# A two-layer transformer on one core: a third bank pair for the gate layer, openings that use idle PSUM banks, and selection's first loads issued inside the stage before it

## The chip, the cores and the metric

One core of one Trainium2 chip runs the whole program. The metric is the device time of one execution in microseconds (us), lower is better. A measurement of this kernel can tell some 0.2% (4 us) from no change.

## What is computed

A tensor x of 8 batches x 512 rows x 256 channels, float32, passes through two layers.

```
xn = layernorm(x)
x  = x + attention0(xn) + ffn0(xn)       # causal, 16 heads of 16, keys and values from a latent of 64
xn = layernorm(x)                        # ffn0: silu(w1 x) * (w2 x) -> gelu(h1 .) -> gelu(h2 .) -> w3, 1024 hidden
x  = x + attention1(xn) + ffn1(xn)       # attention1: no mask, a position bias per head from a table
# ffn1, per group of 16 rows: for each of 64 experts pick the row with the largest logit (controller),
#   inner = relu(f1[expert] row + bias), inter = f2[expert] inner, and add inter back to the picked row
```

Products are made of float32 values split in a rounded high part and a low part (the rest), each a float32r operand.

## The kernel before, in words

The program is a row of five stages, each one block in which every engine has its own instruction stream: attention of layer 0 (`latent_attention`), its feed-forward (`layers`), attention of layer 1 (`biased_attention`), selection (`choose`) and the experts with the final sum (`apply`). A stage begins on all engines once the one before has ended on all of them. The tiles of a stage lie in SBUF over those of earlier stages.

**Attention stages.** Both run a list written out by hand, `STEADY`: 32 steps with events placed in them (`placed`), offset so that a turn holds parts of three batches. Each engine walks the list in the same order and emits its own part of each event. Per batch: the normalized rows are turned by TensorE (`x_turn`), split in high and low (`xh`, `xl`), stored for later stages by SP, multiplied with the weights (`latent` and `qk` in layer 0, four `qk` products in layer 1), and the queries and keys split again into `parts`. SP copies these with six DMAs per group of four heads (`stack`) into `stacks`, from which the score products read. A score is made twice: once for its maximum (`score`, read by VectorE), once for the exponential (`prob`). TensorE's outputs rotate over three slots of two PSUM banks.

- Layer 0, start of a batch (lines 364 to 376, 449 to 466, 319 to 326): ScalarE copies the slot to `x_full` (L368), VectorE rounds it into `xh` (L452), GpSimd subtracts to get `xl` (L321). The queries and keys go the same way through `qk_full`: L375, L463, L324. The third engine of each chain releases the next product or SP's `stack` DMAs (L286).
- Layer 1, start of a batch: the two `x_turn` (L1066) and the four `qk` (L1058) all go through one bank, `single`, since the three slots are in use by the batch before. ScalarE rounds out of it (L941, L947), VectorE subtracts (L1003, L1006), and only then may TensorE write the next one. In the opening batch no earlier batch uses the three slots.

After the `stack` DMAs of two groups SP issues the load of the next batch's rows, `x_load` (L272, L875).

**Feed-forward.** `pe_batch` issues for each of eight blocks of 128 hidden units a gate product and an up product of 8 matmuls in all (L1290), into one of two bank pairs, `gates[o % 2]`, `ups[o % 2]`. Before block o it waits for `gate_done` of block o - 2. ScalarE takes the tanh (L1240), VectorE forms `gated` (L1261) and `full` (L1266, `gate_done`), ScalarE rounds it (L1244, L1247), GpSimd makes the low part (L1232). Two hidden layers of 8 x 16 matmuls (L1320) and the output product (L1366) follow. Banks 0, 1 hold gates, 2, 3 ups, 4 to 7 are free in the gate layer, 4, 5, 2, 3 serve the hidden layers, 6, 7 the output. In batch 0 ScalarE also rounds the weights as they arrive (L1448). In the last batch TensorE computes layer 1's bias table beside the gate layer; its first product waits for the load of `c_fir` (L1183).

**Selection.** Loads of the controller and four constants are issued by ScalarE, those of `xh`, `xl`, `xn` of a batch by SP, at the start of the stage. For each batch: logits (six matmuls, L1989), tie added, maximum and `perm` on VectorE (L1953, L1956, L1960), turned by TensorE (L1996), masked blocks (L1970), and the selecting products (L2009, L2010) from `th` and `tl`, the high and low part of `xn` (ScalarE L1931, GpSimd L1908). The stage of attention 1 ends with ScalarE waiting until its last store of the attention output has landed.

Of the kernel before, what the change touches and what calls it, by code (L numbers as in the profile page):

```python
# [96 lines left out]
def latent_attention(nc, x_d, out_d, xh_d, xl_d, w, c, sems, front):  # L97
# [4 lines left out]
    with ExitStack() as ctx:  # L102
# [163 lines left out]
        with nc.Block() as block:  # L266
# [47 lines left out]
            def _(pool):  # L314
                def emit(kind, b, n, i):
                    if kind == "ln_rstd":
                        wait(pool, eps_done, 1, b)
                        nc.gpsimd.tensor_tensor(rstd[:], var_eps[:], power[:], ALU.pow).then_inc(rstd_ready.sem, 1)
                    if kind == "x_low":
                        wait(pool, xh_ready, 1, b)  # L320
                        pool.tensor_tensor(xl[:], x_full[:], xh[:].bitcast(F32), ALU.subtract).then_inc(xl_ready.sem, 1)  # L321
# [20 lines left out]
            def _(act):  # L342
# [21 lines left out]
                def emit(kind, b, n, i):  # L364
                    if kind == "x_copy":
# [6 lines left out]
                    if kind == "qk_copy":  # L372
                        wait(act, qk_ps, n + 1, b)
                        wait(act, low_ready, n, b)
                        act.copy(qk_full[:], slot("qk", n)[:]).then_inc(qk_copied.sem, 1)  # L375
                        if n == 1 and opening(b):
                            more_high_weights()
# [35 lines left out]
            def _(dve):  # L413
# [18 lines left out]
                def emit(kind, b, n, i):  # L432
# [16 lines left out]
                    if kind == "x_high":  # L449
# [9 lines left out]
                    if kind == "qk_high":  # L459
# [4 lines left out]
                        if n == 1 and opening(b):  # L464
                            more_low_weights()
# [169 lines left out]
def biased_attention(nc, x_d, out_d, xh_d, xl_d, xn_d, w, c, sems, used, x_stored):  # L635
# [4 lines left out]
    with ExitStack() as ctx:  # L640
# [5 lines left out]
        def sem(name, per=0, grant=0, unit=1):  # L646
# [34 lines left out]
        consts_in, w_in = sem("consts_in", unit=16), {n: sem(f"w_in_{n}", unit=16) for n in names + ("o",)}  # L681
        bias_in = [sem(f"bias_in{g}", unit=16) for g in range(QUADS)]
        blank, keyed, ones_ready, w_high, w_ready = \
            sem("blank"), sem("keyed", unit=16), sem("ones_ready"), sem("w_high"), sem("w_ready")
        x_loaded, x_saved = sem("x_loaded", 1, unit=16), sem("x_saved", 2, unit=16)
        xn_saved = sem("xn_saved", 1, unit=16)
        stats_done, moments_done, xn_ready = sem("stats_done", TT), sem("moments_done", TT), sem("xn_ready", TT)
        shift_ready = sem("shift_ready", 1)
        eps_done, rstd_ready = sem("eps_done", 1), sem("rstd_ready", 1)
        xt_ps, xh_ready, xl_ready = sem("xt_ps", KD), sem("xh_ready", KD), sem("xl_ready", KD)  # L690
        v_ps, v_ready = sem("v_ps", 1), sem("v_ready", 1)
        qk_ps, high_ready, low_ready = sem("qk_ps", 4), sem("high_ready", 4), sem("low_ready", 4)
        stack_in = [sem(f"stack_in{g}", 6, unit=16) for g in range(QUADS)]
        tops_in = [sem(f"tops_in{g}", 2, unit=16) for g in range(QUADS)]
        a_ps, a_max = sem("a_ps", STEPS), sem("a_max", STEPS)
        m_ps, tops_ready = sem("m_ps", QUADS), sem("tops_ready", QUADS)
        b_ps, p_exp = sem("b_ps", STEPS), sem("p_exp", STEPS)
        p_copied, p_pooled, p_added = sem("p_copied", STEPS * 3 // 4), sem("p_pooled", STEPS * 3 // 4), sem("p_added", STEPS // 4)
        value_ps, o_copied, ot_ps = sem("value_ps", QUADS * TT), sem("o_copied", QUADS), sem("ot_ps", QUADS)
        inv_ready, mix_ready = sem("inv_ready", QUADS), sem("mix_ready", QUADS)  # L700
        mt_ps, mh_ready, ml_ready = sem("mt_ps", KD), sem("mh_ready", KD), sem("ml_ready", KD)
        out_ps, out_ready = sem("out_ps", 1), sem("out_ready", 1)
        out_saved = sem("out_saved", 1, grant=1, unit=16)
        held_sp, held_dve = sem("held_sp"), sem("held_dve")


        STEADY = []
        def later(s):
# [1656 lines left out]
```

## Time and profile before

| | us |
|---|---|
| three runs | 2061.07, 2060.01, 2056.81; median 2060.01 |
| profiled execution, its own time | 2058.57 |
| span of its profile | 2056.8 |
| TensorE busy, VectorE, ScalarE, GpSimd | 1773.8 (86%), 1148.1, 1063.8, 983.4 |
| attention 0 | 0 to 496 |
| feed-forward | 496 to 1187, a batch of the middle six in 83 |
| attention 1 | 1192 to 1857, a batch in some 78 |
| selection | 1857 to 1920 |
| experts and sum | 1921 to 2057 |

The stages are the stretches between the last instruction of one block and the first of the next in the timeline. Busy times are of the span; TensorE's clock is given in each window as the share that was granted (1.00 is 2.4 GHz, 0.50 is 1.2 GHz). A row of the timeline gives start, duration, engine, line, operation, output and inputs, how many were merged, and in brackets the idle time of the engine before it with what ended that.

### The profile page before, as it was taken

What the parts mean: (1) busy time and instruction counts of PE and PEld (TensorE: products, weight loads), DVE (VectorE), ACT (ScalarE), POOL (GpSimd) and SP (SyncE); (2) the same over time, 40 slices, a digit from 0 to 9 for tenths busy, and PEclk for the clock granted to TensorE, in tenths of its full rate; (3) what the DMA queues carried; (4) which work ended last, traced back from release to release, by engine and by line L of the source; (5) the groups of instructions that cost most, each with busy time, mean ns of one, the idle gap of its engine ahead of it and who ended that gap; (6) DMA issues with size and microseconds to landing.
All of it is one profiled execution on the core that took longest, in us unless ns stands there. A gap on an engine that the chain in (4) does not pass through costs nothing. (4 is left out here: it accounts for less than half of the span.)

```text
span 2056.8 us, 34075 instructions
## 1 busy us (share of the span) xinstructions
PE 1773.8 (86%) x11015; PEld 1141.0 (55%) x11015; DVE 1148.1 (56%) x2519; ACT 1063.8 (52%) x1455; POOL 983.4 (48%) x739
## 2 busy tenths in 40 slices
PE   4888888887999999999997958878878878866999
PEld 2455555544878788787885833334334334325566
DVE  5666666662253353443533358877877877935335
ACT  1555555555432232222322218877877877964542
POOL 3444444432343434434342427776766876954202
PEclk7999999998999999999998959989989989977999
DMA  3333332325420111110201362132132222107346
GB/s 111 94 104 96 94 102 84 96 58 165 150 72 24 56 54 48 56 47 33 79 23 45 115 193 85 57 80 83 60 80 84 62 72 82 32 11 277 122 152 212
DMA packets 119236, 182.53 MB, mean 89 GB/s; under 512 B 14197, under 2 KB 73077, under 8 KB 119162
## 3 DMA queue, kind: packets, MB, share of 16 engines
q1 hardware_dynamic: 109228, 170.45, 27.2%
q10 hardware_dynamic: 9296, 9.05, 1.3%
q0 software_dynamic: 640, 2.10, 0.3%
q8 instruction: 42, 0.69, 0.1%
q14 instruction: 30, 0.25, 0.0%
HBM read 90.72 MB, written 39.91 MB: 64 GB/s over the span
## 5 line engine op out<-in xcount | busy, mean ns | idle before, releaser
L808 POOL TENSOR_TENSOR l_prob<-l_prob,l_bias 128x1024 f32<-128x1024 f32 x192 | 452.2, 2375 | 147.5 <-ACT l_prob L960 146.6
L1232 POOL TENSOR_TENSOR f_hl<-f_full,f_hh 128x512 fp32r<-128x512 f32 x192 | 247.9, 1291 | 426.2 <-DVE f_hh L1270 271.2
L1019 DVE CUSTOM_DVE_ANT_0 l_slot<-l_slot,l_bias 128x512 f32<-128x512 f32 x512 | 340.8, 716 | 52.0 <-PE l_slot L1093 50.0
L963 ACT ACTIVATE l_prob<-l_prob 128x1024 f32<-128x1024 f32 x256 | 271.1, 1071 | 0.0
L472 DVE TENSOR_REDUCE l_peak<-l_slot 128x2 f32<-128x256 f32 (+3 forms) x256 | 206.3, 821 | 107.3 <-PE l_slot L564 105.0
L1320 PE MATMUL f_ps<-f_hh,f_hi_h 128*128 128x512 f32 x1024 | 259.9, 390 | 1.5 <-ACT f_hh L1244 1.1
L1320 PE MATMUL f_ps<-f_hl,f_hi_h 128*128 128x512 f32 x1024 | 258.3, 389 | 0.0
L388 ACT ACTIVATE l_prob<-l_slot 128x1024 f32<-128x1024 f32 (+3 forms) x256 | 174.7, 705 | 97.9 <-PE l_slot L583 95.2
L1320 PEld LDWEIGHTS f_ps<-f_hh,f_hi_h 128*128 128x128 f32 x1024 | 192.1, 188 | 44.1 <-ACT f_hh L1244 2.1
L1320 PEld LDWEIGHTS f_ps<-f_hl,f_hi_h 128*128 128x128 f32 x1024 | 192.2, 188 | 39.9
L960 ACT COPY l_prob<-l_slot 128x1024 f32<-128x1024 f32 x192 | 194.7, 1014 | 35.7 <-PE l_slot L1109 34.9
L1252 ACT ACTIVATE f_full<-f_ps,f_h_s 128x512 f32<-128x512 f32 x128 | 86.8, 684 | 235.2 <-PE f_ps L1320 216.2
L334 POOL TENSOR_SCALAR_AFFINE_SELECT l_prob<-l_prob 128x256 f32<-128x256 f32 x256 | 105.2, 418 | 210.2 <-ACT l_prob L388 207.4
L1270 DVE CAST f_hh<-f_full 128x512 fp32r<-128x512 f32 x128 | 62.1, 485 | 256.3 <-ACT f_full L1252 255.2
L1093 PE MATMUL l_slot<-l_stacks 63*128 63x512 f32 x512 | 120.7, 471 | 47.8 <-DVE l_prob L808 23.5
L1123 PE MATMUL l_o_bank<-l_prob,l_vals 128*32 128x512 f32 x1024 | 157.1, 690 | 4.5 <-ACT l_prob L963 4.5
L1109 PE MATMUL l_slot<-l_stacks 64*128 64x512 f32 x512 | 135.4, 527 | 22.3 <-DVE l_peak L1019 16.2
L1109 PEld LDWEIGHTS l_slot<-l_stacks 64*128 64x128 f32 x512 | 51.7, 200 | 140.5 <-DVE l_peak L1019 98.3
L559 PE MATMUL l_slot<-l_stacks 63*128 63x256 f32 (+2 forms) x512 | 98.6, 382 | 32.7 <-ACT l_prob L388 17.6
L583 PE MATMUL l_slot<-l_stacks 64*128 64x256 f32 (+2 forms) x512 | 109.8, 428 | 11.0 <-DVE l_peak L472 4.0
L1240 ACT ACTIVATE f_tanh<-f_ps,f_gate_s 128x512 f32<-128x512 f32 x64 | 43.9, 687 | 138.3 <-PE f_ps L1290 138.3
L597 PE MATMUL l_o_bank<-l_prob,l_vals 128*32 128x512 f32 (+3 forms) x1024 | 97.9, 454 | 11.1 <-POOL l_prob L334 9.7
(210 smaller groups left out, 2827.0 us busy)
## 6 DMA issues: line engine op xcount, KB each, us to landing
l_stacks<-l_parts SPq DMA_DIRECT2D x384, 128.0 KB, 2.6
attn<-l_out_sb ACTq DMA_DIRECT2D x16, 512.0 KB, 2.9
f_raw<-in_L_ffn_h_w SPq DMA_DIRECT2D x16, 512.0 KB, 4.1
f_raw<-in_L_ffn_h_w SPq DMA_DIRECT2D x32, 256.0 KB, 2.6
e_w<-in_L_ffn_f SPq DMA_DIRECT2D x32, 256.0 KB, 2.9
l_bias<-ext SPq DMA_DIRECT2D x16, 448.0 KB, 8.1
l_x_in<-in_L_attn_x SPq DMA_DIRECT2D x8, 512.0 KB, 3.8
xh<-l_xh SPq DMA_DIRECT2D x8, 512.0 KB, 2.6
```

Of the source, the lines that this page charges most:

```text
L388: act.activation(prob[:, n // 2 % RING, 2 * pr:2 * pr + 2, j * P:T], slot(kind, n)[:, :, j * P - q0:wide], ACT.Exp).then_inc(p_exp.sem, 1)
L472: dve.tensor_reduce(peak[:, g, :, pr, t], slot(kind, n)[:, :, 0:(t + 1) * P], AX_X, ALU.max)\
L583: ins = pe.matmul(out[:, a, 0:wide], stacks[r, 1, 2 * g + pr, j * P:(j + 1) * P], stacks[r, 0, 2 * g + pr, q0:T], start=True, stop=True)
L808: return eng.tensor_tensor(probs(n), src, bias[:, h:h + 2, j * P:j * P + T], ALU.add)
L960: act.copy(probs(n), slot(kind, n)[:]).then_inc(p_copied.sem, 1)
L963: act.activation(probs(n), probs(n), ACT.Exp).then_inc(p_exp.sem, 1)
L1019: ins = dve.tensor_tensor_reduce(src, src, bias[:, 4 * g + 2 * pr + a, t * P:t * P + T], 1.0, 3 * NEG, ALU.add, ALU.max, peak[:, g, a, pr, ...
L1093: ins = pe.matmul(out[:, a], stacks[r, 0, 2 * g + pr, t * P:(t + 1) * P], stacks[r, 1, 2 * g + pr, ::-1], start=True, stop=True)
L1109: ins = pe.matmul(out[:, a], stacks[r, 1, 2 * g + pr, j * P:(j + 1) * P], stacks[r, 0, 2 * g + pr, ::-1], start=True, stop=True)
L1123: ins = pe.matmul(o_bank[32 * a:32 * a + 32, :], vals_sb[:, v0:v0 + 32], prob[:, n % RING, a], start=(j == 0), stop=(j == TT - 1), skip_gr ...
L1232: pool.tensor_tensor(t.hl[layer % 2][:, o], t.full[:, n % 2], t.hh[layer % 2][:, o].bitcast(F32), ALU.subtract).then_inc(self.h_lo.sem, 1)
L1320: ins = pe.matmul(t.hidden[n % 4][:], t.hi[m][:, k, cut], src[layer % 2][:, k], start=first and k == 0, stop=last and k == KH - 1, skip_gr ...
```

## The change

1. Gate layer: three pairs of banks (the third is banks 4, 5); the wait is for block o - 3; the hidden layer's first product waits for block 5 of the gate layer; the bias table's products move from banks 4, 5 to 6, 7.
2. Attention 1, opening batch only: the two `x_turn` write into the two banks of slot 2, the four `qk` into the four banks of slots 0 and 1, without waiting for one another. The first score waits until all four `qk` have been split.
3. Attention 0, opening batch only: ScalarE rounds straight out of PSUM into `xh` and `parts`, VectorE subtracts straight out of PSUM. GpSimd's `x_low` and `qk_low` and the copies to `x_full` and `qk_full` are left out there.
4. Selection: SP issues the controller, the first batch's `xh`, `xl`, `xn` and the constants at the end of its stream of attention 1, after the last `v` copy and the last `stack` DMAs; VectorE splits the controller there too. The wait for the last store moves from the end of attention 1 to the start of selection's ScalarE and the end of its SP. Tiles `xh`, `xl`, `xn` of selection become one per slot and lie in another order.

```diff
 # latent_attention
-                    if kind == "x_copy":
+                    if kind == "x_copy" and opening(b):
+                        wait(act, xt_ps, 1, b)
+                        act.copy(xh[:], slot("x_turn", 0)[:]).then_inc(xh_ready.sem, 1)
+                    elif kind == "x_copy":
...
+                    if kind == "x_high" and opening(b):
+                        wait(dve, xh_ready, 1, b)
+                        dve.tensor_tensor(xl[:], slot("x_turn", 0)[:], xh[:].bitcast(F32), ALU.subtract)\
+                           .then_inc(xl_ready.sem, 1)
+                        wait(dve, xl_ready, 1, b)
+                        dve.sem_inc(xt_full.sem, 1)
...
+                    if kind == "qk_high" and opening(b):
+                        wait(dve, high_ready, n + 1, b)
+                        dve.tensor_tensor(parts[:, n, 0:4:3], slot("qk", n)[:], parts[:, n, 1:3].bitcast(F32),
+                                          ALU.subtract).then_inc(low_ready.sem, 1)
 # biased_attention
+    def bank(kind, n, b):
+        if not opening(b):
+            return single[:]
+        return slots[2][:, n] if kind == "x_turn" else slots[n // 2][:, n % 2]
...
                     if kind == "x_turn":
-                        claim(SINGLE, 1, kind, n, i)
+                    if not opening(b):
+                        claim(SINGLE, 1, kind, n, i)
...
+                    if n == 0 and opening(b):
+                        wait(pe, low_ready, 4, b)
...
             clears(sp, used)
+            sp.wait_ge(v_ready.sem, v_ready.at(1, B - 1))
+            for g in range(QUADS):
+                sp.wait_ge(stack_in[g].sem, stack_in[g].at(6, B - 1))
+            next_opening.sp(sp)
...
-                act.wait_ge(out_saved.sem, out_saved.at(1, B - 1))
...
+            next_opening.dve(dve)
 # Layers
-            if o >= 2:
-                pe.wait_ge(self.gate_done.sem, self.gate_done.at(o - 1, i))
-            two = [t.gates[o % 2][:], t.ups[o % 2][:]]
+            if o >= 3:
+                pe.wait_ge(self.gate_done.sem, self.gate_done.at(o - 2, i))
+            two = [t.gates[o % 3][:], t.ups[o % 3][:]]
...
+                if n == 0:
+                    pe.wait_ge(self.gate_done.sem, self.gate_done.at(KH - 2, i))
...
-        t.gates, t.ups, t.hidden, t.outs = psum[0:2], psum[2:4], psum[4:6] + psum[2:4], psum[6:8]
+        t.gates, t.ups, t.hidden, t.outs = psum[0:2] + psum[4:5], psum[2:4] + psum[5:6], psum[4:6] + psum[2:4], psum[6:8]
...
-        table = BiasTable(nc, sb, f.sem, *bias, c, [psum[4], psum[4], psum[5]],
+        table = BiasTable(nc, sb, f.sem, *bias, c, [psum[6], psum[6], psum[7]],
 # choose
+        def open_sp(sp):
+            sp.dma_start(w_raw[:], controller.rearrange("(k p) n -> p k n", p=P)).then_inc(w_in.sem, 16)
+            load_rows(sp, 0, 0)
+            sp.dma_start(xn[0][:], xn_d[0]).then_inc(xn_in[0].sem, 16)
+            for dst, src in ((tie, "c_tie"), (group, "c_group"), (ident, "c_ident"), (parity, "c_parity")):
+                sp.dma_start(dst[:], c[src]).then_inc(consts_in.sem, 16)
...
             @block.scalar
             def _(act):
-                act.dma_start(w_raw[:], controller.rearrange("(k p) n -> p k n", p=P)).then_inc(w_in.sem, 16)
-                for dst, src in ((tie, "c_tie"), (group, "c_group"), (ident, "c_ident"), (parity, "c_parity")):
-                    act.dma_start(dst[:], c[src]).then_inc(consts_in.sem, 16)
+                act.wait_ge(opening_of.last_saved.sem, opening_of.last_saved.at(1, B - 1))
```

## Rows read from the trace of the kernel before

**Rows 1.** Windows, one feed-forward batch: us, busy by engine, granted clock, DMA share, GB/s

```profile
670.00:753.00 83.00, 81.41 (x386) 67.30 (x385) 33.59 (x65) 23.90 (x39) 33.29 (x25) 1.00 0.16 49
```

**Rows 2.** Timeline of TensorE in the gate layer of batch 1

```profile
586.85 1.09 PE L1290 MATMUL f_ps<-f_xl,f_hi_w 128*128 128x512 f32 x4
...
591.14 1.20 PE L1290 MATMUL f_ps<-f_xl,f_hi_w 128*128 128x512 f32 x4 [0.47 <-DVE f_full L1266]
...
603.92 1.96 PE L1320 MATMUL f_ps<-f_hh,f_hi_h 128*128 128x512 f32 x7
```

**Rows 3.** Line 1290, batches 1 to 6, idle of matmul and weight load: us, times

```profile
  DVE f_full L1266: 26.5, 36
```

**Rows 4.** Timeline of ScalarE and VectorE, block 0 of that gate layer

```profile
588.89 0.69 ACT L1240 ACTIVATE f_tanh<-f_ps,f_gate_s 128x512 f32<-128x512 f32 x1 [11.77 <-PE f_ps L1290]
...
590.33 0.75 DVE L1266 SCALAR_TENSOR_TENSOR f_full<-f_ps,f_both_s,f_gated 128x512 f32<-128x512 f32 x1
```

**Rows 5.** Timeline of TensorE, end of batch 0's gate layer

```profile
518.37 0.47 PE L1320 MATMUL f_ps<-f_hh,f_hi_h 128*128 128x512 f32 x1 [1.06 <-ACT f_hh L1244]
```

**Rows 6.** Timeline of TensorE, the last batch's gate layer

```profile
1107.61 0.51 PE L1183 MATMUL f_ps<-f_wpos,f_coeffs 4*101 4x16 f32 x2 [14.51 <-DMA f_out_sb<-c_fir]
```

**Rows 7.** Timeline of VectorE, GpSimd and TensorE in attention 0's opening, the x split

```profile
14.23 0.69 DVE L452 CAST l_xh<-l_x_full 128x1024 fp32r<-128x1024 f32 x1 [1.83 <-ACT l_x_full L368]
...
15.01 2.34 POOL L321 TENSOR_TENSOR l_xl<-l_x_full,l_xh 128x1024 fp32r<-128x1024 f32 x1 [5.36 <-DVE l_xh L452]
...
17.49 0.76 PE L513 MATMUL l_m_bank<-l_xl,l_wc 128*128 128x512 f32 x1 [4.34 <-POOL l_xl L321]
```

**Rows 8.** Timeline there: first stack DMAs, first score, next x; a VectorE sum from PSUM

```profile
27.24 7.91 SPq L286 DMA_DIRECT2D l_stacks<-l_parts  x12
...
33.48 0.58 PE L559 MATMUL l_slot<-l_stacks 63*128 63x256 f32 x2 [8.59 <-issue]
...
39.43 0.43 DVE L436 BATCH_NORM_STATS2 l_stats<-l_x_in 128x6 f32<-128x256 f32 x1 [2.54 <-DMA l_x_in<-in_L_attn_x]
...
1821.58 1.23 DVE L808 TENSOR_TENSOR l_prob<-l_slot,l_bias 128x1024 f32<-128x1024 f32 x1 [5.28 <-PE l_slot L1109]
```

**Rows 9.** Timeline of attention 1's opening batch, and one window (columns as Rows 1)

```profile
1194.67 1.11 PE L1066 MATMUL l_single<-l_ident,l_xn 128*128 128x128 f32 x4 [1.40 <-DVE l_xl L1003]
1197.28 0.77 PE L1058 MATMUL l_single<-l_xl,l_wq 128*128 128x512 f32 x1 [1.49 <-DVE l_xl L1003]
...
1201.62 0.77 PE L1058 MATMUL l_single<-l_xl,l_wk 128*128 128x512 f32 x1 [1.45 <-issue]
...
1205.90 7.89 SPq L891 DMA_DIRECT2D l_stacks<-l_parts  x12
...
1214.48 0.69 DVE L1019 CUSTOM_DVE_ANT_0 l_slot<-l_slot,l_bias 128x512 f32<-128x512 f32 x1
...
1218.33 0.43 DVE L990 BATCH_NORM_STATS2 l_stats<-l_x_in 128x6 f32<-128x256 f32 x1
...
1209.00:1213.00 4.00, 2.68 (x6) 1.82 (x6) 0.69 (x1) 0.49 (x1) 0.00 (x0) 0.50 0.75 201
```

**Rows 10.** Timeline across the end of attention 1 and the start of selection

```profile
1853.87 0.39 ACTq L978 DMA_DIRECT2D attn<-l_out_sb  x1
1857.24 0.47 ACTq L1924 DMA_DIRECT2D s_w_raw<-in_L_ffn_controller  x1
...
1863.23 0.77 PE L1989 MATMUL s_ps<-s_xl,s_w_high 128*128 128x512 f32 x1 [10.49 <-DMA s_xl<-yl]
...
1868.53 0.69 DVE L1953 TENSOR_TENSOR s_logits<-s_ps,s_tie 128x512 f32<-128x512 f32 x1 [5.99 <-DMA s_parity<-c_parity]
...
1868.58 2.34 POOL L1908 TENSOR_TENSOR s_tl<-s_xn,s_th 128x1024 fp32r<-128x1024 f32 x1 [31.65 <-DMA s_parity<-c_parity]
...
1869.98 1.49 DVE L1960 TENSOR_TENSOR s_perm<-s_logits,s_best 128x512 f32<-128x512 f32 x1
...
1871.52 1.12 PE L1996 MATMUL s_ps<-s_ident,s_perm 128*128 128x128 f32 x4 [5.39 <-DVE s_perm L1960]
```

More of the change, by code:

```diff
@@ L371, in emit @@
                         act.copy(top[:], m_bank[:]).then_inc(c_top.sem, 1)
-                    if kind == "qk_copy":
+                    if kind == "qk_copy" and opening(b):
+                        wait(act, qk_ps, n + 1, b)
+                        act.copy(parts[:, n, 1:3], slot("qk", n)[:]).then_inc(high_ready.sem, 1)
+                    elif kind == "qk_copy":
                         wait(act, qk_ps, n + 1, b)
@@ L758, in slot @@
-        def slot(kind, n):
-            return slots[[(u[0], u[2]) for u in PAIRED].index((kind, n)) % 3]
-        def there(b):
-            return not isinstance(b, int) or 0 <= b < B
-        def turns(eng, emit):
-            def turn(i):
-                for kind, off, n in STEADY:
-                    if there(i + off):
-                        emit(kind, i + off, n, i)
-            turn(-1)
-            turn(0)
-            with eng.Fori(1, B - 1) as i:
-                turn(i)
-            turn(B - 1)
-            turn(B)
@@ new lines, in biased_attention @@
+    for s in range(STEPS):
+        STEADY += placed[s]
+        STEADY.append(("prob", 0 if s >= LAG else -1, (s - LAG) % STEPS))
+        at = s - LAG - TAKEN
+        STEADY.append(("prob_exp", 0 if at >= 0 else -1, at % STEPS))
+        STEADY.append(("score", 0, s))
+    LAST_READ = {"score": a_max, "prob": None, "v": v_ready, "out": out_ready,
+                 "maxima": tops_ready, "x_turn": xl_ready, "qk": low_ready, "heads_turn": mix_ready, "mix_turn": ml_ready}
+    PAIRED = [e for e in STEADY if e[0] in ("score", "prob", "v", "out")]
@@ new lines, in bank, with there, turns, turn @@
+    def bank(kind, n, b):
+        if not opening(b):
+            return single[:]
+        return slots[2][:, n] if kind == "x_turn" else slots[n // 2][:, n % 2]
+    def there(b):
+        return not isinstance(b, int) or 0 <= b < B
+    def turns(eng, emit):
+        def turn(i):
+            for kind, off, n in STEADY:
+                if there(i + off):
+                    emit(kind, i + off, n, i)
+        turn(-1)
+        turn(0)
+        with eng.Fori(1, B - 1) as i:
+            turn(i)
+        turn(B - 1)
+        turn(B)
```

912 lines of the change are left out of this document (465 added, 447 removed).

## The prediction

> **What bounds the kernel now.** I read the busy shares first, then the granted clock by slices, then the timeline of each place that the diff touches, and for the gate layer the idle time of its line. The five stages run one after the other, so every microsecond saved on the path inside one comes off the whole. In the feed-forward TensorE is the bound: busy 81.41 of 83 us of a batch at a granted clock of 1.00 [rows 1]. What it loses there it loses in the gate layer, waiting for VectorE [rows 2, 3]. The three other edits lie where one batch alone is under way, and nothing else covers a wait: a chain over three engines at the opening of attention 0 [rows 7], one PSUM bank passed from hand to hand at the opening of attention 1 [rows 9], and loads that are issued only once the stage before has ended [rows 10].
>
> **Part 1, the gate layer.** Eight blocks of 8 matmuls take from 586.85 to 603.92, 17.07 us [rows 2]. Blocks 0 and 1 run without a wait. Their 16 matmuls end 0.47 before 591.14, after 3.82 us, and the first four of them take 1.09 [rows 2]; so twelve more cost 2.73, 0.228 each, a block of eight is 1.83 and eight blocks are 14.6. The stage thus loses 2.4 us, in three waits (36 entries for matmul and weight load together are 18 waits in six batches [rows 3]). A wait is the chain of block o: tanh 0.69 from 588.89, `gated`, `full` up to 591.08, and TensorE starts at 591.14 [rows 2, 4]. From the end of a block's products to `gate_done` that is 2.3 us. With two pairs it must fit in one block, 1.83; with three it has two blocks, 3.66, and 1.3 us to spare. Do the other engines keep up with a block every 1.83? ScalarE has the tanh (0.69) and a rounding of the same size, VectorE 0.69 and 0.75, each under 1.5, so the wait goes and none takes its place. The new wait ahead of the hidden layer asks for block 5, which was done over a microsecond before TensorE comes to it: nothing. The start of the hidden layer waits for the rounding of block 6 and does so at the same distance from the end of the gate layer. Batches 1 to 6: 6 x 2.4 = 14.6 us.
> Batch 0 gives nothing. ScalarE rounds weights between the tanhs there, and TensorE stands 1.06 us waiting for its rounding at the end of the gate layer [rows 5]; reaching that wait earlier makes it longer. The last batch gives nothing either: TensorE waits 14.51 us for the table of `c_fir` [rows 6], a load issued behind the store of batch 6, and the waits saved ahead of it are taken back by it. The table's move to banks 6 and 7 costs nothing: their reader, the output of batch 6, is done before block 3. Bounds: 13.0 (a tenth lost in new small waits) and 14.8.
>
> **Part 2, attention 0's opening.** Now a copy on ScalarE ends where VectorE starts at 14.23; then 0.69 for the cast, 2.34 on GpSimd, and TensorE starts at 17.49 [rows 7]. After, ScalarE's copy is the rounding, of the same size, and VectorE subtracts from PSUM: 1.23 for 1024 elements, one operand from PSUM [rows 8]. It ends at 15.46, TensorE starts at 15.6: 1.9 us less. The same exchange for the queries and keys takes 1.9 more off the moment at which SP issues its stack DMAs, 27.24 now [rows 8]. Scores need the first six of these (33.48, 6.24 after the first issue), and the load of the next rows is issued behind all twelve and is waited for at 39.43 [rows 8]. Both hang on SP's start, so the whole stage moves by up to 3.8. GpSimd was idle else, and what is left out there covers nothing. Bounds 3.2 (the products between lie at 1.2 GHz, and the clock may rise no earlier than it did) and 3.9. I take 3.7.
>
> **Part 3, attention 1's opening.** The second `x_turn` waits 1.40 for the bank and follows at once after [rows 9]. The first `qk` then starts 1.4 earlier, at 1195.9; its own wait of 1.49 for the second split stays. From one `qk` to the next is 4.34, of which 1.45 idle [rows 9]. SP's first stack DMAs need `qk` 0 and 1: 1.4 + 1.45 and some 0.3 because the second is no longer behind a drained pipeline, 3.2 us: 1202.7 instead of 1205.90. From there it is as in attention 0: scores 6.24 later at 1208.9, VectorE's first maximum at about 1209.8 instead of 1214.48, 4.7 earlier. But the next rows are issued behind twelve DMAs of 7.89 in all and land 4.3 after that (39.43 against 27.24 + 7.91 [rows 8]), at 1214.9, and VectorE wants them after three scores. So VectorE, ahead of plan, waits for them, and the stage moves by what separates 1214.9 from 1218.33 [rows 9], 3.4. The new wait of the first score for all four splits costs nothing: these are done by 1208.5, the stack DMAs land later. Behind it in TensorE's queue stands nothing else of that batch. I take 3.5; bounds 3.0 and 4.7.
> The granted clock is 0.50 in this stretch and TensorE was busy 2.68 of 4 us [rows 9]. With the four products in one run it may rise within them, which takes up to 1 us more off. The Trainium skill, in "TensorE: Matmul & The Clock Gate", section "Why this matters for your kernels", says that idle gaps between bursts of matmuls send the array back to the low clock; by that rule the run without gaps would be shortened and part 3 would be 4.3 in place of 3.5.
>
> **Part 4, selection's loads.** Now: last store issued at 1853.87, next stage's first issue at 1857.24, logits at 1863.23 (waiting for `xl`), VectorE at 1868.53 (waiting for the last constant, `parity`), turn of `perm` at 1871.52 [rows 10]. After, batch 0's data and the constants are in SBUF long before, as SP is free once the last stacks are made, and the stage turns over when ScalarE has issued the store: 1853.87 + 0.39 and some 0.4, 1854.7. Six logit products at 1.2 GHz are 2.9 (4.34 - 1.45 [rows 9]): 1857.6. VectorE then needs 1.45 up to `perm` (1868.53 to 1869.98 [rows 10]): 1859.0.
> Here a new order counts. ScalarE's `th` waits for the last store, which lands at about 1857, so GpSimd's `tl` runs from some 1858.1 to 1860.5 (2.34 [rows 10]). In the trace `perm` beside it took 1.49 and ended at 1871.47, 0.55 after GpSimd's 1870.92. I let it end 0.55 after GpSimd again, 1861.0, and the turn starts at 1861.1: 10.4 us earlier. The Trainium skill, "SBUF — State Buffer", section "SBUF: two separate sides", says that a VectorE instruction with two SBUF inputs and a GpSimd one exclude each other by a lock on a shared port pair; this trace agrees with its 1.49 for `perm`, and without such a lock this part would be 11.2.
> What is late next: batch 1's `xh`, `xl` and `xn`, issued by SP from 1854.7 on, behind one another and with the first expert weights. They have 6.4 us to the turn at 1861.1; today the first two loads of the stage, with the constants beside them, take from 1857.24 to 1863.23 [rows 10], 6.0. So they are just in time, and `xn` is wanted last. SP's seven new issues (about 0.4 us each [rows 10]) lie in its idle time; VectorE's split of the controller stands behind its last instruction while TensorE and ScalarE still work. Both cost nothing; were that cover gone, 3 and 0.8 us. Bounds: 8.5 (batch 1 late by 2) and 13 (logits still at the high clock, `perm` ahead of GpSimd). I take 10.4.
>
> **Sum.** 14.6 + 3.7 + 3.5 + 10.4 = 32.2 us. The profiled execution took 2058.57, so 2026.4 of its kind; it lies 1.4 under the median of the runs, 2060.01, so 2027.8 for a median.
>
> **Rivals.**
> A. *The gate's waits move* instead of going: ScalarE or GpSimd falls behind, TensorE waits at the third pair or at the hidden layer. For it: three engines follow one another. Against: each has under 1.5 of work in 1.83 [rows 4]. Half of the gain would be left: 2035.
> B. *Selection is bound by batch 1's loads.* Traffic then sets the pace at its start, and part 4 gives 5 rather than 10: 2033. For it: `xl` and `parity` are waited for today [rows 10]. Against: 1.5 MB fewer are in the queue.
> C. *Slower.* Attention 1 falls into another rhythm, since its opening hands VectorE work 3 to 5 us earlier than the loads for the next batch, with TensorE at 0.50 of its clock [rows 9] for longer in each of the seven batches that follow. It decides from 4.6 us per batch on (32.2 / 7); at 6 the time is 2070. Nothing in the profile shows a batch that depends on how the first began.
> Within the forecast, with a chance of 0.3: the clock rises inside the four `qk` products, which is worth up to 1 us, 2027 instead of 2027.8.
> D. *The openings' edits do not act* (another wait ends at the same time, such as weights or the bias load): parts 2 and 3 give nothing, 2035.
>
> **How the numbers follow.** Forecast 0.76, A 0.07, B 0.09, C 0.02, D 0.06. The range takes in the bounds, 8.5 + 13.0 + 3.0 + 3.2 = 27.7 to 13 + 14.8 + 4.7 + 3.9 = 36.4, that is 2032.3 to 2023.6, widened by the runs' own spread of 2 to each side (2056.81 to 2061.07), and on the slow side up to A, B and D: 2021 to 2035. Faster by over 0.2% (4 us; what a measurement of this kernel can tell from no change): all but C, 0.97. Within 0.2%: 0.01. Slower: 0.02.
>
> **What would show it.** Line 1290 without waits for `full` in batches 1 to 6 and a batch in 80.6 instead of 83; TensorE's first latent product at 15.6 and SP's stacks at 23.4; four `qk` products in one run, stacks 3 to 4 us sooner after the start of attention 1; no wait for a constant in selection, and 7 us from the last store's issue to the turn of `perm` instead of 17.6. It would be wrong if L1290 waits for anything in those batches, if attention 1's batches are longer than today, or if selection's second batch waits for its `xh` or `xn`.

## The result, and the profile after

Six runs of the changed kernel took 2048.42, 2039.23, 2040.68, 2049.53, 2040.46 and 2039.73 us, median 2040.57; six of the kernel before beside them had a median of 2059.43. The ratio is 0.9916 (95% interval 0.9900 to 0.9932): faster by 0.84%. Between the medians it is 18.9 us; the ratios here and below differ a little from those of the medians. Forecast were 32.2 us and 2027.8, with a range of 2021 to 2035. So 13 us are missing, and the median lies 5.6 us outside the range. The profiled execution is the one of 2048.42, span 2046.7. Five of the executions behind the tables below were in a slower state of the chip, 5 to 54% longer, and all medians leave them out.

The four places that the diff touches do what it says. First windows of both kernels: a feed-forward batch of the changed one, then all of attention 1 in the kernel before (us, busy by engine, granted clock, DMA share, GB/s).

```profile
670.00:750.48 80.48, 80.48 (x386) 67.67 (x385) 33.62 (x66) 23.97 (x39) 33.35 (x25) 1.00 0.16 50
```

```profile
1190.00:1860.00 670.00, 526.00 (x2912) 235.76 (x2912) 495.21 (x1320) 508.06 (x589) 462.58 (x203) 0.88 0.25 73
```

TensorE is busy for the whole batch, where it was for 81.41 of 83 [rows 1]. The timeline of TensorE in the gate layer of batch 1 answers to [rows 2]:

```profile
588.45 1.09 PE L1326 MATMUL f_ps<-f_xl,f_hi_w 128*128 128x512 f32 x4
...
602.08 1.08 PE L1326 MATMUL f_ps<-f_xh,f_hi_w 128*128 128x512 f32 x4
602.99 1.96 PE L1356 MATMUL f_ps<-f_hh,f_hi_h 128*128 128x512 f32 x7
```

Eight blocks now take 14.54 us (588.45 to 602.99), forecast 14.6, and no row between bears a wait. Next come the openings: attention 0's subtraction, first stacks and first score, as in [rows 7, 8], then attention 1's, as in [rows 9].

```profile
14.23 1.22 DVE L460 TENSOR_TENSOR l_xl<-l_slot,l_xh 128x1024 fp32r<-128x1024 f32 x1 [1.83 <-ACT l_xh L369]
...
15.61 0.77 PE L534 MATMUL l_m_bank<-l_xl,l_wc 128*128 128x512 f32 x1 [2.45 <-DVE l_xl L460]
...
23.61 6.61 SPq L286 DMA_DIRECT2D l_stacks<-l_parts  x10
...
29.78 0.58 PE L580 MATMUL l_slot<-l_stacks 63*128 63x256 f32 x2 [6.65 <-issue]
...
1177.99 1.94 PE L1098 MATMUL l_slot<-l_ident,l_xn 128*128 128x128 f32 x8 [5.12 <-PEq L1643]
1181.42 0.77 PE L1089 MATMUL l_slot<-l_xl,l_wq 128*128 128x512 f32 x1 [1.49 <-DVE l_xl L1033]
1181.99 1.05 PE L1089 MATMUL l_slot<-l_xh,l_wq 128*128 128x512 f32 x2
...
1187.94 0.62 PE L1089 MATMUL l_slot<-l_xh,l_wk 128*128 128x512 f32 x2
1194.43 1.65 PE L1128 MATMUL l_slot<-l_stacks 63*128 63x512 f32 x6 [5.87 <-DMA l_stacks<-l_parts]
...
1200.42 0.43 DVE L1020 BATCH_NORM_STATS2 l_stats<-l_x_in 128x6 f32<-128x256 f32 x1 [1.06 <-DMA l_x_in<-x]
```

TensorE's first latent product is at 15.61 instead of 17.49, the first stack DMA at 23.61 instead of 27.24, the first score at 29.78 instead of 33.48: 3.7 us. In attention 1 the four `qk` follow one another without a wait, and VectorE waits 1.06 us for the next rows, as forecast. And the turn into selection, as in [rows 10]:

```profile
1855.78 0.39 ACTq L1009 DMA_DIRECT2D attn<-l_out_sb  x1
...
1856.80 0.77 PE L2052 MATMUL s_ps<-s_xl,s_w_high 128*128 128x512 f32 x1 [2.15 <-PEq L894]
...
1860.31 2.34 POOL L1979 TENSOR_TENSOR s_tl<-s_xn,s_th 128x1024 fp32r<-128x1024 f32 x1 [20.48 <-ACT s_th L2000]
...
1861.25 1.95 DVE L2023 TENSOR_TENSOR s_perm<-s_logits,s_best 128x512 f32<-128x512 f32 x1
...
1863.26 0.85 PE L2059 MATMUL s_ps<-s_ident,s_perm 128*128 128x128 f32 x4 [3.56 <-DVE s_perm L2023]
```

From the last store's issue to the turn of `perm` it takes 7.48 us, where it took 17.65 (1853.87 to 1871.52).

Yet look at the last store itself: 1855.78, later than the 1853.87 of [rows 10], though attention 1 began 14 us earlier. So the loss lies inside attention 1. ScalarE's copies of a batch's output (line 974 before, 1005 after) are good marks. Before, the first is at 1351.8 and the eighth at 1852.8, 501.0 us apart; after, 1335.6 and 1854.7, 519.1 apart. The first six follow one another every 78.5 us before and every 82.2 after (82.16 is (1746.4 - 1335.6) / 5). No line of that loop's steady batches was changed. The granted clock of all of attention 1 does not give the cause away: here is the same window after, with the same 0.88 (the columns are those of the second window above). Over the five steady batches alone, from the first output copy to the sixth, it is 0.91 before and 0.89 after, a difference to which the experiments come back.

```profile
1190.00:1860.00 670.00, 523.15 (x2886) 235.85 (x2886) 491.74 (x1315) 506.50 (x584) 459.80 (x199) 0.88 0.24 71
```

### The profile page after: what moved, and what is told of

Its sections match the earlier page's. It is cut to its first block and busy times, and to the rows that moved or that the text cites. A ratio compares the mean times of both kernels' runs of the same rounds, so it can differ in the third digit from the quotient of the medians.

```text
span 2046.7 us, 34076 instructions
## 1 busy us (share of the span) xinstructions
PE 1773.9 (87%) x11015; PEld 1149.2 (56%) x11015; DVE 1150.4 (56%) x2519; ACT 1066.1 (52%) x1455; POOL 978.8 (48%) x736
## 5 line engine op out<-in xcount | busy, mean ns | idle before, releaser
L1128 PE MATMUL l_slot<-l_stacks 63*128 63x512 f32 x512 | 125.0, 488 | 61.5 <-DVE l_prob L835 27.4
L1144 PEld LDWEIGHTS l_slot<-l_stacks 64*128 64x128 f32 x512 | 52.8, 204 | 138.7 <-DVE l_peak L1049 85.1
L1128 PEld LDWEIGHTS l_slot<-l_stacks 63*128 63x128 f32 x512 | 54.4, 209 | 101.1 <-DVE l_prob L835 41.7
```

Of the source, the lines that this page charges most:

```text
L1128: ins = pe.matmul(out[:, a], stacks[r, 0, 2 * g + pr, t * P:(t + 1) * P], stacks[r, 1, 2 * g + pr, ::-1], start=True, stop=True)
L1144: ins = pe.matmul(out[:, a], stacks[r, 1, 2 * g + pr, j * P:(j + 1) * P], stacks[r, 0, 2 * g + pr, ::-1], start=True, stop=True)
```

## Experiments

My first theory, T1, came from the low stretches of the granted clock, which in the changed kernel fall on other products of a batch: the loop keeps a rhythm with the clock, and whatever shifts its start throws it into another one. T2: the new opening of attention 1 itself makes the batches longer. T3: changed addresses or the early loads do. The mean batch in the tables is a fifth of the time from the first to the sixth output copy, in the run's profile. A median of the kernel before taken beside each group stands with it. "First to last" is the distance of those eight output copies in the run's profile.

**One part at a time** (before: 2059.19). Each run has the lines of one part of the diff, and the lines before for the rest.

> Only part 1 of the change (the gate layer on three pairs of banks); openings and selection as before. All theories: the gate stage is shorter by 6 x 2.5 = 15 us. Theory T1 (the attention loops keep a rhythm with the ups and downs of the granted clock, and what is shifted ahead of them can throw them into another one): attention 1, whose own code is that of before, starts 15 us earlier and may now take 80 to 82 us a batch where it took 78.2 (up to 18 us lost of the 15 won; 2042 to 2062), with a clock dip more per batch; if it keeps 78.2, 2045. Rival T2 (the new opening of attention 1 by itself puts the loop into the worse rhythm): 2044 to 2046, batches of 78.2 us. Rival T3 (selection's early loads or the changed addresses slow attention 1): the same 2044 to 2046.

> Only part 2 (attention 0's opening split from PSUM). All theories: first score product and first layer-norm wait 3.6 us earlier. T1: the batches' spacing in attention 0 changes by a us or two each, so that 0 to 3.6 us of it is left at that stage's end, and attention 1 may fall into either of its spacings (78.2 or 81.9 us): anything from -4 to +18 us against before, and runs of two kinds. T2 and T3: the 3.6 us stay, 2056, with attention 1 at 78.2 us a batch.

> Only part 3 (attention 1's opening batch round six score banks). T2: the batches of attention 1 take 81.9 us as in the changed kernel, and the whole is slower than before by some 14 us (2073). T1: the spacing may be either; first store 3 to 4.7 us earlier. T3: batches of 78.2 us, 2056.

> Only part 4 (selection's constants loaded in the drain of attention 1). T1: nothing ahead of selection's own loads is moved, so attention 1 keeps its 78.2 us a batch; the stretch from the last out copy of attention 1 to the end of the span is shorter by 10 to 12 us, 2048 to 2050. T2: the same. T3: the changed addresses alone give attention 1 batches of about 82 us, so that the whole is no faster than before (2055 to 2065).

| run | median us | ratio (95%) | mean batch of attention 1 | first to last |
|---|---|---|---|---|
| gate_only | 2047.42 | 0.9944 (0.9931 to 0.9957) | 78.7 | 500.7 |
| open0_only | 2072.59 | 1.0056 (1.0037 to 1.0074) | 81.4 | 516.5 |
| open1_only | 2057.46 | 0.9986 (0.9976 to 0.9996) | 79.0 | 503.2 |
| select_only | 2050.64 | 0.9955 (0.9942 to 0.9968) | 78.6 | 501.1 |

The second part, the opening of attention 0, makes the kernel 13 us slower by itself, and does so in attention 1, 1.2 ms after its own instructions. That rules out T2 and T3: part 4 leaves the batches alone, and part 3 makes them 0.5 longer, not 3.7. It left T1 standing, for the wrong reason.

**Without the second part, and with a filled or delayed attention 1** (before: 2059.30). `three_parts` has `OPEN0` off. The other two edits are these; `warm` issues two products at each of the first places and four at each of the other two. Those that write to `single` also wait until that bank's last reader is done, which the lines shown leave out.

```diff
 # warm: after each of the first eight scores, ahead of each wait for tops_in, ahead of ml_ready
+pe.matmul(out, wq[:, 0, 0, 0:P], wv[:, 0, 0], start=True, stop=True)
 # delay: ScalarE, opening batch of attention 1, before the first copy of x_turn; three times
+act.copy(o_sb[:, 0], wq[:, 0].bitcast(F32).rearrange("p k d -> p (k d)")).then_inc(lagged.sem, 1)
+act.wait_ge(lagged.sem, m + 1)
```

> The change without its second part (attention 0's opening as before). The three parts alone gave -11.8, -1.7 and -8.6 us, in sum -22.1. Additive parts: 2037, 3.5 us under the changed kernel although one improvement is taken out of it. T1 (rhythm of attention 1 with the granted clock): the batches of attention 1 may take 78 to 79 us (then 2033 to 2038) or 81 to 82 (then 2048); with the second part's own 3.6 us at the start missing, any time under the changed kernel's 2040.6 speaks for T1 against T2, since the opening of attention 1 is still the new one.

> The kernel before, with products whose result nobody reads put into TensorE's idle time in attention 1 from its second batch on: two of 256 columns behind each score product of the first eight steps of a batch, four ahead of the wait for each quad's maxima, four ahead of the output product. They cost 48 x 0.11 = about 5 us of TensorE's time a batch where they don't fit into waits. T1: what makes a batch 78 to 82 us is the stretches at the low clock, so with these filled the granted clock of attention 1 rises from 0.88 to 0.95 or more and the batches fall to 74 to 77 us: 10 to 25 us less, 2035 to 2050. If the low clock is only a by-product and VectorE and ScalarE set the batch, the clock rises and the time stays or grows: 2059 to 2080.

> The changed kernel with the same filling products. T1: its 81.9 us a batch and those of the kernel before fall to the same 74 to 77 us, so that the four parts show nearly their whole sum: 2005 to 2030, 28 to 32 us under the filled kernel before. T2 (the new opening makes the batches longer by itself): still 3 to 4 us a batch slower than the filled kernel before.

> The changed kernel with ScalarE held up by three copies (about 2 us) between attention 1's first turn product and the copy of it, nothing else. Without a rhythm: 2 us slower, 2042.5. T1: the loop meets the clock's fall at another place, and the time moves by something else than 2 us: from 10 us faster to 10 us slower, with another spacing of the batches than 81.9 us, or with runs spread wider than the changed kernel's.

| run | median us | ratio (95%) | mean batch | first to last |
|---|---|---|---|---|
| three_parts | 2032.33 | 0.9880 (0.9857 to 0.9902) | 78.5 | 500.1 |
| warm_before | 2083.83 | 1.0110 (1.0086 to 1.0133) | 81.7 | 519.6 |
| warm_after | 2065.85 | 1.0034 (1.0016 to 1.0052) | 85.1 | 536.2 |
| delay3_after | 2042.54 | 0.9922 (0.9900 to 0.9944) | 80.8 | 513.3 |

Three parts are 8 us faster than all four. The filling is a miss for T1: in the kernel before the clock of the steady batches (1430 to 1745) rose from 0.91 to 0.93, and the batches grew by 3 us. The 260 filling products in the trace kept TensorE busy for 58.3 us, 0.22 each where I had set 0.11, and it stood idle ahead of some of them (8.2 us in all, nearly all of it until VectorE had written `l_mix`); which of the two made the batches longer was not taken apart. Filled before and filled after still lie 3.4 us a batch apart; but their clocks in that window, 0.93 and 0.90, differ as well, so this pair alone doesn't decide. And the delay of 1.92 us made the whole 2.0 us longer.

**Delays with and without the second part** (before: 2063.44). `all_wait0` puts six such copies ahead of attention 0's first rounding; the others put two, five and six into attention 1. T4 is new: it is the second part's code, and not when it runs. (T5, tried against it further down: it is something else that the second part leaves behind.)

> The changed kernel, all four parts, with ScalarE held up by six copies (6 x 0.64 = 3.8 us by the copies of the last delayed run) between attention 0's first turn product and its first rounding, so that its first score product stands where it stood before the second part (33.5 us) while the second part's code stays. T1 (what counts is where the loops meet the clock's falls, hence when they start): the batches of attention 1 go back to 76.6 to 80.3 us and the whole to that of the three parts, 2030 to 2038, that is 3 to 10 us faster for 3.8 us of added waiting. Rival T4 (the second part's code, its addresses or its order slows something later by itself, whenever it runs): 2044, batches of 80.5 to 82 us.

> The three parts (without attention 0's new opening) with ScalarE held up by two copies (1.3 us) at the start of attention 1. T4: 1.3 us slower than the three parts, 2033.6, same batches of 76.6 to 80.3 us. T1: another meeting with the clock; batches of 80 to 82 us are possible though the second part is absent, 2030 to 2050.

> The same with five copies (3.2 us). T4: 2035.5, same batches of 76.6 to 80.3 us. T1: 2030 to 2050, and the three times at 0, 1.3 and 3.2 us of delay don't lie on the line of slope 1.

> The changed kernel, all four parts, with six copies (3.8 us) at the start of attention 1; three copies gave 2042.5 with batches of 80.5 to 81.1 us. T4: 2044.4, batches of 80.5 to 82 us. T1: the phase may be that of the fast rhythm: 2033 to 2050, batches of 76.6 to 80.3 us possible though the second part is in.

| run | median us | ratio (95%) | mean batch | first to last |
|---|---|---|---|---|
| all_wait0 | 2047.02 | 0.9922 (0.9907 to 0.9937) | 81.2 | 513.5 |
| three_wait2 | 2033.46 | 0.9858 (0.9839 to 0.9877) | 78.3 | 501.8 |
| three_wait5 | 2035.11 | 0.9860 (0.9841 to 0.9879) | 79.0 | 503.2 |
| all_wait6 | 2048.26 | 0.9917 (0.9896 to 0.9938) | 81.9 | 518.6 |

T1 has fallen. Without the second part, delays of 0, 1.3 and 3.2 us give 2032.3, 2033.5 and 2035.1 and batches of 78.3 to 79.0. (That the three times lie on a line of slope 1 shows little: the kernel before took 4 us more beside the last two than beside the first.) With it, no delay brings a batch below 80.8. Attention 0's first score back near its old place (33.07) didn't help.

With that I read what the idle time of VectorE in attention 1 is put down to, kernel by kernel. Waits of VectorE from 1190 to 1860, total us, times, longest; first `three_parts`, then the changed kernel:

```profile
DVE l_slot L1056 <- PE l_slot L1136: 55.2, 33, 5.1
...
DVE l_slot L1056 <- issue: 0.7, 3, 0.4
```

```profile
DVE l_slot L1049 <- PE l_slot L1128: 62.9, 35, 5.5
...
DVE l_slot L1049 <- issue: 9.4, 3, 3.4
...
DVE l_prob L835 <- issue: 3.9, 5, 0.9
```

"Issue" is time in which the engine waited for nothing that the profile shows. Every kernel with the second part up to here has five such gaps in line 835 (3.2 to 3.9 us in all) and most have some of 3 us before line 1049; none without it has more than 0.7 us in all. In VectorE's timeline the gaps of 3 us stand at one place, where a turn of its loop ends and the next one begins. The loop has six turns, so it jumps back five times. The changed kernel:

```profile
1418.90 0.73 DVE L1049 CUSTOM_DVE_ANT_0 l_slot<-l_slot,l_bias 128x512 f32<-128x512 f32 x1
...
1422.63 0.70 DVE L1049 CUSTOM_DVE_ANT_0 l_slot<-l_slot,l_bias 128x512 f32<-128x512 f32 x1 [2.94 <-issue]
...
1425.05 1.23 DVE L835 TENSOR_TENSOR l_prob<-l_slot,l_bias 128x1024 f32<-128x1024 f32 x1 [0.88 <-issue]
```

TensorE's score for the row at 1422.63 had begun at 1420.33. In `three_parts` the first of the same two rows of VectorE starts 0.69 us after its score, and the second right behind the copy of the maxima:

```profile
1573.57 0.50 PE L1136 MATMUL l_slot<-l_stacks 63*128 63x512 f32 x2 [1.23 <-ACT l_prob L996]
```

```profile
1574.26 0.70 DVE L1056 CUSTOM_DVE_ANT_0 l_slot<-l_slot,l_bias 128x512 f32<-128x512 f32 x1 [1.31 <-PE l_slot L1136]
...
1575.52 0.27 DVE L1065 CAST l_tops<-l_single 16x128 fp32r<-16x128 f32 x1
1575.75 1.22 DVE L839 TENSOR_TENSOR l_prob<-l_slot,l_bias 128x1024 f32<-128x1024 f32 x1
```

The totals put down to "issue" are too small, for the profile names TensorE for some of these gaps. Read at the row itself, whatever is named, a long gap is there at all five jumps of every kernel with the second part. These are the ranges over all twenty profiles, the later ones included; the loop's place is explained below, and so is why the kernels fall into four groups by it.

| loop begins at | profiles | gap at the jump, us | second gap, before the addition (line 835) |
|---|---|---|---|
| 829, 845, 848 | 11 | 1.31 to 1.37 | none put down to "issue" |
| 832 | 7 | 2.94 to 3.78 | 0.60 to 0.93 |
| 833 | 1 | 2.87 to 2.95 | 0.70 to 0.72 |
| 840 | 1 | 4.20 to 4.45 | none |

Behind the sixth turn, where nothing jumps back, it is 1.09 in all twenty. In the changed kernel the gaps sum to 19.7 us and in the kernel before to 7.1. So 12.6 of the 18.1 us by which attention 1 is longer stand in these rows. The rest goes with the clock. From the first to the sixth output copy the granted clock is 0.91 or 0.92 in all ten kernels of the first group that have no filling products. It is 0.91 in `delay3_after`, whose attention 1 is the least lengthened of the others, 0.87 to 0.89 in the other seven, and lowest in `all_pad8`, the longest. That the gaps bring the clock down, and that the lower clock costs the rest, fits these numbers but was not tried by itself.

One more row of the page differs: the packets of the second instruction queue. It is the page's section on DMA queues (packets, MB, share), kernel before first, changed kernel second.

```profile
q8 instruction: 42, 0.69, 0.1%
q14 instruction: 30, 0.25, 0.0%
```

```profile
q14 instruction: 55, 0.45, 0.1%
```

So the changed kernel fetches 0.20 MB more of instructions, 25 packets for five jumps back. In the built program VectorE's loop of attention 1 is 268 instructions long. It begins at number 829 of VectorE's queue in the kernel before, and at 832 in the changed one, because the second part puts three bare `sem_inc` on that queue. ScalarE's loop is 172 long and lies one place earlier, GpSimd's is 52 long and lies three places earlier, and TensorE's, 412 long, did not move.

**Moving the loop's code** (before: 2058.86; for `all_pad8` and `all_pad16` 2059.59). The fillers cost nothing, VectorE idles there.

```diff
 # VectorE, attention 1, ahead of turns(dve, emit); 3, 1, 13, 8 or 16 times
+dve.sem_inc(lagged.sem, 1)
 # all_moved: the three increments of the second part go from VectorE to GpSimd, for x:
-wait(dve, xl_ready, 1, b)
-dve.sem_inc(xt_full.sem, 1)
+wait(pool, xl_ready, 1, b)
+pool.sem_inc(xt_full.sem, 1)
 # and the two of qk_copied behind low_ready in the same way
```

> The three parts (no new opening in attention 0) with three increments of a semaphore that nobody waits for, put on VectorE's queue right ahead of its turns in attention 1. VectorE idles there, so they cost nothing themselves; with them its loop of attention 1 (268 instructions) begins at instruction 832 of its queue, where it begins with the second part, and not at 829. T4 as it now reads (VectorE stands still for 3 us with nothing that it waits for, where its loop of attention 1 turns back, in every kernel with the second part and in none without, because of where the loop's code lies): the idle time put down to issue comes up here too, batches of 80.5 to 82 us, 2040 to 2048. T5 (it is something else that the second part leaves behind, on ScalarE, GpSimd or in the data): no change, 2032, batches of 76.6 to 80.3 us.

> All four parts with one such increment: the loop begins at 833. T4, if only certain places are bad (832 is the first multiple of 4, of 16 and of 64; 829 leaves 1, 13 and 61): the gap of 3 us goes if a multiple of 4 or more is what makes it, then 2028 to 2033 with batches of 76.6 to 80.3 us; if the gap grows with the distance from a boundary, it is the same as at 832 and the time stays at 2040 to 2048. T5: 2040 to 2048.

> All four parts with thirteen such increments: the loop begins at 845, which leaves the same rest as 829 for 4, 8 and 16. T4 with blocks of up to 16 instructions: no gap, 2028 to 2033. T4 with larger blocks: the gap may stay, 2040 to 2048. T5: 2040 to 2048.

> All four parts; the three bare increments that the second part puts on VectorE's queue (one behind the rounding of x, two behind that of q and k) are done by GpSimd, which has nothing to do there. VectorE's loop of attention 1 begins at 829 again. T4: no gap at the turn of the loop, batches of 76.6 to 80.3 us, and the whole has the second part's own gain on top of the three parts': 2027 to 2031, the fastest kernel of this study. T5: 2040 to 2048.

> All four parts with eight increments ahead of VectorE's loop of attention 1, which begins at 840, a multiple of 4 and of 8 but not of 16. So far the gap at the loop's turn is there with a start at 832 and 833 and absent at 829 and 845. If what is bad is a start at or just behind a multiple of 16: no gap, 2022 to 2032. If a start on any multiple of 4 or 8 is bad: gap of 3 us, 2040 to 2048.

> The same with sixteen increments: the loop begins at 848, a multiple of 16 but of nothing larger. If the places repeat every 16 instructions, it is 832 over again: gap of 3 us, 2040 to 2048. If they repeat only every 32 or 64, or if any start past 840 is good: no gap, 2022 to 2032.

| run | loop begins at | median us | ratio (95%) | mean batch | first to last | q14 packets |
|---|---|---|---|---|---|---|
| all_moved | 829 | 2032.06 | 0.9879 (0.9863 to 0.9895) | 78.1 | 500.6 | 30 |
| three_pad3 | 832 | 2046.75 | 0.9940 (0.9922 to 0.9958) | 81.9 | 518.0 | 55 |
| all_pad1 | 833 | 2044.85 | 0.9932 (0.9914 to 0.9950) | 81.9 | 517.9 | 55 |
| all_pad8 | 840 | 2051.30 | 0.9955 (0.9938 to 0.9973) | 84.4 | 530.3 | 56 |
| all_pad13 | 845 | 2024.78 | 0.9841 (0.9818 to 0.9864) | 78.9 | 501.7 | 31 |
| all_pad16 | 848 | 2030.61 | 0.9862 (0.9845 to 0.9879) | 78.7 | 500.9 | 31 |

T4 holds and T5 falls. Three increments that nobody waits for, with no line of the second part, bring the gaps, the 25 packets and the long batches; three increments taken off VectorE's queue, with the second part in, take all of it away. GpSimd's loop lies where it was before in `three_pad3`, which is slow, and where the second part puts it in `all_pad13`, which is fast, so it is not that one. VectorE's waits in `three_pad3`, same view as above:

```profile
DVE l_prob L859 <- issue: 3.9, 5, 0.9
DVE l_slot L1083 <- issue: 3.0, 1, 3.0
```

And one gap of `all_pad8`, where it stands in one piece:

```profile
1507.28 0.70 DVE L1083 CUSTOM_DVE_ANT_0 l_slot<-l_slot,l_bias 128x512 f32<-128x512 f32 x1 [4.40 <-issue]
```

My guesses at which places are bad were wrong both times: 840 is bad and 848 is not, so it is no rule of multiples of 4, 8 or 16. Over all twenty profiles of this case, those that begin at 829, 845 or 848 have 30 or 31 packets on that queue, and those at 832, 833 or 840 have 55 or 56. Good places lie on both sides of the bad ones: whatever the bad stretch is, it lies within 830 to 844, and the bad places found span 832 to 840.

The Trainium skill, "Runtime: NRT & Kernel Launch", section "Instruction fetch mechanics", says that an engine other than TensorE holds two blocks of 256 instructions, prefetches in sequence only, and that a branch to a block it no longer holds must fetch it first. By that rule a loop of 268 fits in two blocks unless it begins in the last 11 places of a block, when it lies in three; then each turn fetches again. This case agrees: the bad places found span 9, and the good ones 829 and 845 lie 16 apart, so a stretch of 11 has room between them. The second gap says where a block ends, if the instructions are counted in the built program. In the kernels that begin at 832, VectorE still executes its instruction 839 (the copy of the maxima) and then stands before 842 (the addition). In the one at 833 it executes 840 and stands before 843. So a block begins at 841 or 842. Then, by the same rule, the bad places are 830 to 840 or 831 to 841, which agrees with all six that were tried; with a start at 840 the jump and the end of the block nearly coincide, and there the gap is in one piece. This is an estimate from the gaps and the rule; no run has a start at 830, 831, between 834 and 839 or between 841 and 844.

## Why the prediction was wrong

**The parts.** Each did nearly what its working said. Part 1: 2.53 us a batch (17.07 to 14.54 for the eight blocks), 15.2 for six, forecast 14.6; by itself it gave 11.8 between medians. (The forecast's "6 x 2.4" is 14.4, and 17.07 less 14.6 is 2.47 and not 2.4; either slip is 0.2 us.) Part 2: 3.7 at the first score, as forecast. At the end of attention 0 (its last output copy) ten profiles with the second part and no delay there have a mean of 494.8, and nine without it 497.8; so about 3.0 of the 3.7 stay. That is uncertain by about 1 us, since single profiles range over 7 us in either group (492.0 to 499.4 and 494.0 to 501.6); in the two profiles of before and after alone attention 0 ends 1.5 later. Part 3: from the end of the feed-forward's products to VectorE's first statistics of the next rows it was 31.24 us (1187.09 to 1218.33) and is 27.55 (1172.87 to 1200.42), 3.7 less, forecast 3.5; by itself it gave 1.7 between medians, and its batches took 79.0 in place of 78.5; why is open. The clock rose inside the four `qk` products, which the forecast had at 0.3: a pair at line 1089 takes 1.05 us at 1181.99 and the last one 0.62, and the granted clock was 0.50 from 1181.4 to 1184.1 and 0.98 from there to 1189. It went with 3.7 and not with the 4.3 that the prediction worked out for it. Part 4: 10.2 from store to turn, forecast 10.4; `perm` ended 0.55 after GpSimd (1863.20 and 1862.65), as in the working; by itself it gave 8.6. Parts 1, 3 and 4 taken singly add up to 22.1, together (`three_parts`) they gave 27.0; the 5 us between are not explained.

**The sum.** With VectorE's loop in a good place all four parts gave 26.8, 34.1 and 29.0 us (`all_moved`, `all_pad13`, `all_pad16`, each against the kernel before beside it), 30.0 in the mean, where 32.2 were forecast. All three medians, mean 2029, lie in the range. So the sum was sound to 2 us in the mean of the three. They lie 7 us apart, though, more than the 4 us that count as a change, and no run tells why.

**The step that failed** is the one from the parts to the whole: "every microsecond saved on the path inside one comes off the whole". The sum has four terms and puts the steady batches of attention 1 at no change, without a reason beyond "Nothing in the profile shows a batch that depends on how the first began". They went from 78.5 to 82.2 us. The term missing belongs to part 2, which counts the subtraction and says nothing of what else the edit adds to VectorE's queue. (That "what is left out there covers nothing" on GpSimd stands.) Its three `sem_inc` cost no time where they stand. They shift all of VectorE's later code by three places, and the longest of its loops then stands still at each of its five jumps back, with 25 packets more on the instruction queue. In the profiles attention 1 became 18.1 us longer that way (519.1 against 501.0); between medians the change gave 18.9 us in place of those 30.0, so the loop's place cost about 11. The pairs of kernels that differ in little else give 8 (`all_moved` against the changed kernel) and 14 (`three_pad3` against `three_parts`).

**The rivals.** C had the right place and the right sign, by luck: the batches of attention 1 are longer, by 3.7 us, under the 4.6 from which it would have decided, and longer batches there were one of the prediction's own signs of being wrong. C's mechanism was not what happened: the openings' earlier work, with the low clock there, leaves the batches at 78 to 79 us in every kernel whose loop lies well and whose TensorE is not filled. A, B and D did not occur. The sign was right, and the kernel is faster by more than 0.2%, which had a chance of 0.97; the range was too narrow because all its terms were of instructions, and none of where the code lies.

The changed kernel's own runs spread over 10 us and `all_pad8`'s over 12.5, while `select_only`'s five lie within 1.6. The longer runs of the changed kernel have the lower mean granted clock (0.930 and 0.928 at 2048.42 and 2049.53, 0.933 to 0.938 in the four others). So clock and time move together from run to run by some us; what set the two kernels apart is the loop's place, and the clock at most carried a part of it. How much of the spread comes from the clock stays open.

## What to carry to other kernels

Before an edit ahead of a long hardware loop, count the instructions that it adds to each engine's queue, waits and bare increments too, and look how long the loops behind it are: one of 268 instructions on VectorE made attention 1 13 to 29 us longer in the profiles by where it began (513.3 to 530.3 against 500 to 503, in the kernels without filling products). If a stage that was not touched becomes slower, compare the packets of the instruction queues on the page and the idle time put down to "issue" at the loop's turn before thinking of the clock; both stood in the two profiles of before and after. Then move the code by a few fillers and see, or put bookkeeping increments on a queue with short loops (`all_moved`). The fastest kernel here is `all_pad13`, the changed kernel with thirteen fillers: 2024.78 us (0.9841).

## Not expected of the hardware

- A turn of VectorE's loop stood still for 3.6 to 4.5 us, at one place or split in two, where it else waits 1.3, when the loop's 268 instructions began at 832, 833 or 840 of its queue, and not when they began at 829, 845 or 848. The instruction queue carried 25 packets more, 0.20 MB, that is 8 KB each.
- Products of 256 columns with weights of their own kept TensorE busy for 0.22 us each in attention 1, twice the 0.11 that I had set. Filling its idle time with them raised the granted clock of the steady batches from 0.91 to 0.93 in the kernel before, which became 24 us slower.
- The load of the table `c_fir` holds TensorE for 14.51 us in the kernel before [rows 6] and for 15.44 in the changed one, and the granted clock is 0.50 right after it in both. To remove it was not tried; it is TensorE's longest single wait that the changed kernel has left.
